# A fused recurrent-attention and mixture-of-experts layer: group 0 enters the pipeline half by half

## The reference, cut to what matters

```
# layer 1, over each group
h = layernorm(x);  h = h / max(norm(h), 1e-12) * sqrt(256) * gamma
q, kv, a = split(h @ w_qkva.T, 3);  a = sigmoid(a)
y[t] = a[t] * y[t-1] + kv[t];       x = x + q * y
# layer 2, top-2 routing to 8 experts, capacity 256 per group and expert
logits = layernorm(x) @ router_w     # softmax, two best, positions by cumsum
hidden = gelu(rows @ w0[e]) * (rows @ w1[e]);  x = x + sum of gate * (hidden @ wo[e])
```

## Time and profile before

| what | before |
|---|---|
| median of three runs | 1752.66 us (1750.37 to 1752.70) |
| the profiled execution's own time | 1755.55 us |
| its span | 1753.8 us |
| busy PE / DVE / ACT / POOL | 1693.2 / 833.6 / 713.8 / 388.6 us |
| mean granted TensorE clock | 0.977 |

### The profile page before, as it was taken

How to read it: one execution, slowest core, us unless ns; L and a number is a source line. 1 busy time by engine, 2 the same in 40 slices (tenths; PEclk the granted TensorE clock), 3 DMA queues, 4 the chain that set the end, 5 groups by cost and what they waited for, 6 DMA issues and landing times.

```text
span 1753.8 us, 25482 instructions
## 1 busy us (share of the span) xinstructions
PE 1693.2 (97%) x10284; PEld 1514.3 (86%) x10284; DVE 833.6 (48%) x1672; ACT 713.8 (41%) x1236; POOL 388.6 (22%) x310
## 2 busy tenths in 40 slices
PE   5989996999999999999999999999999999999997
PEld 4778885989999988899899899899899989989886
DVE  5888875333533354335433453345334533353332
ACT  4556552333533343334433443344333433353332
POOL 3366756411011111111111111111111111111111
PEclk9988986999999999999999999999999999999999
DMA  9356533211411151115111421132113311241111
GB/s 310 131 170 214 194 104 134 59 25 22 116 26 24 25 121 25 25 25 113 33 25 25 97 49 25 25 88 58 25 25 74 72 25 25 53 93 16 34 13 13
DMA packets 112318, 120.76 MB, mean 69 GB/s; under 512 B 14472, under 2 KB 99912, under 8 KB 112200
## 3 DMA queue, kind: packets, MB, share of 16 engines
q1 hardware_dynamic: 87624, 85.29, 16.3%
q0 software_dynamic: 24576, 33.83, 11.3%
HBM read 59.84 MB, written 59.24 MB: 68 GB/s over the span
## 4 chain that ended last, share of the span: by engine, by line
PE 87%; DVE 4%; POOL 4%; ACT 2%; issue 2%; DMA 1%; SPq 0%; POOLq 0%; ACTq 0%
PE bank L1156 53%; PE bank L1172 28%; PE bank L1020 3%; POOL slots L522 2%; PE bank L1096 2%; DVE y L783 1%; POOL pw L506 1%; PE bank L1066 1%; DVE st L803 0%; DVE z L789 0%; PE bank L1056 0%; ACT x2nT L619 0%; POOL sc L510 0%; POOL out L571 0%; ACT xn L594 0%
## 5 line engine op out<-in xcount | busy, mean ns | idle before, releaser
L981 DVE TENSOR_TENSOR y<-bank,sig 128x512 f32<-128x512 f32 (+1 forms) x352 | 243.3, 691 | 571.1 <-PE bank L1156 561.2
L571 POOL DMA_INDIRECT out<-xring x128 | 200.9, 1569 | 1221.4 <-ACT xring L726 1189.8
L709 ACT ACTIVATE hhi<-y 128x512 fp32r<-128x512 f32 (+1 forms) x352 | 222.3, 631 | 525.4 <-DVE y L981 525.4
L1156 PE MATMUL bank<-xThi,whi 128*128 128x512 f32 x1408 | 426.1, 383 | 0.0
L1156 PE MATMUL bank<-xTlo,whi 128*128 128x512 f32 x1408 | 425.4, 382 | 0.0
L1156 PE MATMUL bank<-xThi,wlo 128*128 128x512 f32 x1408 | 423.8, 381 | 0.0
L1172 PE MATMUL bank<-whi,hhi 128*128 128x256 f32 (+1 forms) x1408 | 389.7, 277 | 0.0
L1172 PE MATMUL bank<-wlo,hhi 128*128 128x256 f32 (+1 forms) x1408 | 387.8, 275 | 0.0
L1172 PE MATMUL bank<-whi,hlo 128*128 128x256 f32 (+1 forms) x1408 | 387.4, 275 | 0.0
L984 DVE TENSOR_TENSOR hlo<-y,hhi 128x512 fp32r<-128x512 f32 (+1 forms) x352 | 243.6, 692 | 245.6 <-ACT hhi L709 245.6
L703 ACT ACTIVATE sig<-bank 128x512 f32<-128x512 f32 (+1 forms) x352 | 209.3, 595 | 289.8 <-PE bank L1156 289.8
(11 more groups left out here) (110 smaller groups left out, 1072.0 us busy)
## 6 DMA issues: line engine op xcount, KB each, us to landing
stage<-in_L_ffn_w_kernel SPq DMA_DIRECT2D x160, 128.0 KB, 3.0
slots<-fill SPq DMA_DIRECT2D x32, 520.0 KB, 6.1
xring<-slots SPq DMA_DIRECT2D x32, 520.0 KB, 3.5
stage<-in_L_ffn_wo_kernel SPq DMA_DIRECT2D x80, 128.0 KB, 3.0
xring<-in_L_attn_x SPq DMA_DIRECT2D x16, 512.0 KB, 4.4
out<-xring SPq DMA_DIRECT2D x16, 512.0 KB, 4.1
slots<-rows,sloti POOLq DMA_INDIRECT x128
out<-xring POOLq DMA_INDIRECT x128, 3.8
```

The lines of the kernel that those rows point to most:

```text
L571: pool.indirect_dma_start(out_rows, bass.IndirectOffsetOnAxis(idx, 0), ysb[:, t % 2, j, :], None, compute_op=ALU.add).then_inc(added, 16)
L709: act.activation(hhi[0:n, hc % 3, :], hf[0:n, hc % 2, :], ACT.Copy).then_inc(h_hi, 1)
L981: dve.tensor_tensor(hf[0:n, hc % 2, :], up[hc % 2][1][0:n, :], gel[0:n, hc % 2, :], ALU.mult).then_inc(mul_done, 1)
L1156: last = pe.matmul(lines(up[hc % 2][w][:, :]), (whi, wlo)[wp][:, hc, at:at + P], lines((xThi, xTlo)[xp][:, t % 2, k, :]), start=m == 0 and ...
```

## The change

Group 0's statistics are finished per half: the operands ve of a half are made right behind its bn_aggr, POOL makes a power of 8 columns per half (`powers1_first`), and DVE makes the factors per half (`factors1_first`). In step -1 PE now transposes only half 0 of group 0; half 1 is transposed in step 0, behind `projection(0,0,0)`. Step -1 is written apart for ACT and DVE (`first_step`). DVE takes the statistics of (1,1) in step 0, behind the first recurrence. SP loads the projection weights between the two halves of group 0, ahead of gamma and router. The waits of ACT, DVE and PE for gamma and router stand at their first use. ACT runs one small sigmoid at its start.

```diff
 # SP
             load_x(Turn(0), 0)
+            sync.dma_start(wraw, w_qkva.rearrange("(c p) d -> p c d", p=P)).then_inc(wq_loaded, 16)
             load_x(Turn(0), 1)
             sync.dma_start(gamma[:, :], ...).then_inc(consts_loaded, 16)
             sync.dma_start(router[:, :, :], ...).then_inc(consts_loaded, 16)
-            sync.dma_start(wraw, w_qkva.rearrange("(c p) d -> p c d", p=P)).then_inc(wq_loaded, 16)
 # POOL
+            def powers1_first(h):
+                pool.wait_ge(consts_made, 1)
+                pool.wait_ge(stats1, h + 1)
+                flat = [a[:, h, :, :].rearrange("p k j -> p (k j)") for a in (pw1, ve1, halves)]
+                pool.tensor_tensor(flat[0], flat[1], flat[2], ALU.pow).then_inc(pow1, 1)
...
-                if S:
+                if S and i.value > -2:
                     powers1(i.plus(2))
+                elif S:
+                    powers1_first(0)
+                    powers1_first(1)
 # ACT
-            act.wait_ge(consts_loaded, 32)
+            act.wait_ge(consts_raw, 3)
+            act.activation(nb2[:, 0, 0:1], halves[:, 0, 0, 0:1], ACT.Sigmoid)
...
+            def first_step():
+                normalise1(Turn(0), 0)
+                projection_weights()
+                act.wait_ge(consts_loaded, 32)
+                split1(Turn(0), 0)
+                normalise1(Turn(0), 1)
+                first_weights(0)
+                split1(Turn(0), 1)
+                first_weights(1)
 # DVE
-            dve.wait_ge(consts_loaded, 32)
-            dve.wait_ge(consts_made, 1)
...
-                if h == 1:
+                if g.value == 0:
+                    dve.tensor_scalar(ve1[:, h, 0, :], mv1[:, h, :, 1], LN_EPS, None, ALU.add)
+                    dve.tensor_scalar(ve1[:, h, 1, :], mv1[:, h, :, 1], float(D), None, ALU.mult).then_inc(stats1, 1)
+                elif h == 1:
...
+            def factors1_first(h):
+                dve.wait_ge(pow1, h + 1)
+                ... (the five instructions of factors1, on half h)
...
+            def first_step():
+                factors1_first(0)
+                projection_weights()
+                dve.wait_ge(consts_loaded, 32)
+                split1(Turn(0), 0)
+                factors1_first(1)
+                dve.wait_ge(consts_made, 1)
+                statistics1(Turn(1), 0)
...
                 if B:
                     split1(i, 1)
                     recurrence(i, 0, 0)
+                if i.value == 0:
+                    statistics1(Turn(1), 1)
 # PE
-            pe.wait_ge(consts_loaded, 32)
...
+                if i.value == -1:
+                    transpose1(Turn(0), 0)
+                    return
...
                 if B:
                     projection(i, 0, 0)
+                if i.value == 0:
+                    transpose1(Turn(0), 1)
```

More of the change, by code:

```diff
@@ L228, in build @@
         fac_chain1 = sem("fac_chain1")
+        first_fac_chain1 = sem("first_fac_chain1")
         stats_chain2 = sem("stats_chain2")
@@ L477, in _ @@
                                pattern=[[1, P]], channel_multiplier=-1)
-            pool.memset(halves[:, :, 0, :], -0.5)
+            pool.memset(halves[:, :, 0, :], -0.5).then_inc(consts_raw, 1)
             pool.memset(halves[:, :, 1, :], 0.5)
@@ L500, in first_weights @@
                                    ALU.subtract).then_inc(w_split0, 1)
+            def powers1_first(h):
[3 more added lines that the diff above has]
+                pool.tensor_tensor(flat[0], flat[1], flat[2], ALU.pow).then_inc(pow1, 1)
             def powers1(g):
-                wait(pool, stats1, g, 1, 1)
+                wait(pool, stats1, g, 1, 2)
                 flat = [a[:, :, :, :].rearrange("p h k j -> p (h k j)") for a in (pw1, ve1, halves)]
@@ L589, in normalise1 @@
             def normalise1(g, h):
-                wait(act, fac1, g, 1, 1)
+                if g.value == 0:
+                    act.wait_ge(fac1, h + 1)
+                else:
+                    wait(act, fac1, g, 1, 2)
                 wait(act, t1, g, 2, h)
@@ L644, in step @@
             def step(i):
+                if i.value == -1:
+                    first_step()
+                    return
                 A, B, C, Dg = live(i, 1), live(i, 0), live(i, -1), live(i, -2)
@@ L659, in step @@
                     normalise1(i.plus(1), 0)
-                if i.value == -1:
-                    projection_weights()
                 for hc in first[0:len(first) // 2]:
@@ L735, in _ @@
             dve.sem_inc(mul_done, FREE_MUL)
-            dve.wait_ge(consts_loaded, 32)
-            dve.wait_ge(consts_made, 1)
             in_stats1 = Chain(dve, stats_chain1, 4)
             in_fac1 = Chain(dve, fac_chain1, 4)
+            in_first_fac1 = Chain(dve, first_fac_chain1, 8)
             in_stats2 = Chain(dve, stats_chain2, 4)
@@ L753, in statistics1 @@
                 in_stats1.link(last)
-                if h == 1:
+                if g.value == 0:
+                    dve.tensor_scalar(ve1[:, h, 0, :], mv1[:, h, :, 1], LN_EPS, None, ALU.add)
+                    dve.tensor_scalar(ve1[:, h, 1, :], mv1[:, h, :, 1], float(D), None, ALU.mult).then_inc(stats1, 1)
+                elif h == 1:
                     dve.tensor_scalar(ve1[:, :, 0, :], mv1[:, :, :, 1], LN_EPS, None, ALU.add)
                     dve.tensor_scalar(ve1[:, :, 1, :], mv1[:, :, :, 1], float(D), None, ALU.mult).then_inc(stats1, 1)
+            def factors1_first(h):
+                dve.wait_ge(pow1, h + 1)
+                in_first_fac1.begin(Turn(0), 4 * h)
+                link = in_first_fac1.link
+                link(dve.tensor_tensor(nrm[:, h, :], pw1[:, h, 0, :], pw1[:, h, 1, :], ALU.mult))
+                link(dve.tensor_scalar(rec[:, h, :], nrm[:, h, :], NORM_MIN, None, ALU.max))
+                link(dve.reciprocal(rec[:, h, :], rec[:, h, :]))
+                link(dve.scalar_tensor_tensor(out=sc1[:, h, :], in0=pw1[:, h, 0, :], scalar=float(D) ** 0.5,
+                                              in1=rec[:, h, :], op0=ALU.mult, op1=ALU.mult))
+                dve.scalar_tensor_tensor(out=nb1[:, h, :], in0=mv1[:, h, :, 0], scalar=-1.0, in1=sc1[:, h, :],
+                                         op0=ALU.mult, op1=ALU.mult).then_inc(fac1, 1)
             def factors1(g):
-                wait(dve, pow1, g, 1, 1)
-                in_fac1.begin(g)
+                wait(dve, pow1, g, 1, 2)
+                in_fac1.begin(g.plus(-1))
                 in_fac1.link(dve.tensor_tensor(nrm[:, :, :], pw1[:, :, 0, :], pw1[:, :, 1, :], ALU.mult))
@@ L1060, in route @@
                 wait(pe, x2nT_done, g, 4, 2 * h + 2)
+                if (g.value, h) == (0, 0):
+                    pe.wait_ge(consts_loaded, 32)
                 wait(pe, shifted if h == 0 else routed, g, 1, 0)
```

## The result

| | before | changed |
|---|---|---|
| median of 6 runs, us | 1752.11 (1750.37 to 1753.77) | 1757.63 (1754.81 to 1760.76) |
| profiled execution, own time / span | 1755.55 / 1753.8 | 1757.49 / 1755.8 |
| ratio to before, 95% interval | | 1.003 (1.002 to 1.004) |
| first matmul of the projections, us | 25.80 | 17.87 |
| y(0,0,0), y(0,0,1), first residual start | 30.27, 34.23, 48.15 | 28.20, 37.68, 52.95 |

The changed kernel is slower by 5.5 us, 0.3%. The table's rows show the course: 7.9 us ahead at the first projection (its row on PE begins at 25.80; the 26.15 of the earlier trace rows is where the chain passes to it, behind the transposes), 2.1 ahead at y(0,0,0), 3.5 behind at y(0,0,1), 4.8 behind at the first residual, and 4.3 behind at the first scatter.

The account below looks back on a forecast made before the run. The experts bind PE from 297 us, so the change acts through the chained pipeline ahead. Terms +2.9, +0.4 and +0.9 sum to +4.2 us, 1756.9 us against the median 1752.66; range 1751.8 to 1760.5.

Parts of the forecast that it names:

- Head: Loads, statistics and normalising ahead of PE's projections: projection (0,0,0) starts at 18.2 instead of 26.15, an 8 us win.
- The sigmoid queued behind half 1: ACT's sigmoid waits behind half 1's split and a weight copy; y(0,0,0) starts at 27.5, win down to 2.8 us.
- The wait for the power: DVE's nrm waits for POOL's group 1 power, 0.1 + 2.94 us behind the moved statistics; y(0,0,1) at 35.7 against 34.23.
- The port: DVE's nrm is blocked beside POOL's split of chunk 1 and ends about 1.7 us late; y(0,0,1) then at 37.4.
- No gap on DVE from y(0,1,0) on: DVE works without idling from y(0,1,0) at 41.75 for 9.3 us; first residual at 51.05 against 48.15, +2.9.
- The clock terms: PE's slower clock: +0.4 us in the first projection (5.8 us), +0.9 us for 12 matmuls behind the pause (bounds 0 to 1.9).
- Rival (b): PE's clock falls in the pauses and the first projection stays slow: +7.2 us, 1759.9; chance 0.11.
- The table load: ACT's table load of 1.28 us ahead of normalising goes, by the row; 2.7 by the skill's page, total 1.4 lower.
- The shift arrives: The pipeline has no fixed date, so a shift at about 48 us arrives whole at the end.
- (c): Rival: DVE's wait is covered and the head's 8 us win is kept: 1744.7; chance 0.07.
- (d): Rival: the shift is swallowed by slack between 50 and 100 us: 1752.7; chance 0.06.
- (a): Rival: nrm is not blocked because DVE gets there first; +1.2, +0.4 and +0.2 give 1754.5; chance 0.26.

Follow-up runs that it names:

- the first experiment: The changed kernel with the statistics of (1,1) back in step -1, behind those of (1,0); ratio 0.9976 to the kernel before.
- both lesser terms out: The changed kernel with POOL's split of chunk 1 ahead of group 1's power and 13 more matmuls on PE in the pause; ratio 1.0001 to the kernel before.
- split ahead: The changed kernel with POOL's split of chunk 1 moved ahead of the power of group 1; ratio 1.0007 to the kernel before.
- PE kept busy: The changed kernel with 20 more matmuls on PE into an unused bank, between pa and pkv of block (0,1,0); ratio 1.0011 to the kernel before.
- x first: The changed kernel with the statistics of (1,1) back in step -1 and the projection weights loaded behind both halves of x; ratio 0.9979 to the kernel before.
- the waits alone: The kernel before with only the gamma and router waits moved to first use and ACT's small sigmoid at its start; ratio 0.997.

## Why the prediction was right, point by point

The forecast was 1756.9, the median is 1757.63; +4.2 us was forecast and +5.5 measured. The mechanism is the one that was forecast. That the two times lie only 0.7 us apart is partly luck: the forecast stood on a median of 1752.66 from three runs, six give 1752.11, and the terms were less exact than the total.

- **Head.** Projections at 18.2, measured 17.87. The 26.15 of before, against which the win was counted, is the chain's number; the first matmul began at 25.80. The weights landed by 6.71 (7.0), half 1 by 8.31 (8.5), xn started at 11.32 (11.8). POOL's power of 8 columns takes 1.68 and 1.64 us, inside the bounds, and is hidden.
- **The sigmoid queued behind half 1.** y(0,0,0) at 27.5 plus the clock's 0.4, measured 28.20. Shown by the experiment that puts the sigmoid first: y(0,0,0) at 21.86, against 25.61 in the kernel that it is built on.
- **The wait for the power,** 3.0 us at nrm: measured 3.01. Its removal is the first experiment.
- **The port.** nrm was put at 1.7 us late, from the row at 99.38; it is 1.6 late, and 0.17 us long with the split moved. The same form of stall came back on nb in the experiment with the sigmoid first. Both agree with the rule of the Trainium skill (SBUF — State Buffer, "Who interferes with whom"). That POOL's power does not block agrees with the earlier trace rows and not with that rule: sc and nb of half 0, each of two SBUF tiles, ran at 10.92 and 11.12, beside the power of half 1 (10.55 to 12.19), in 0.16 us each, and xn was not late.
- **No gap on DVE from y(0,1,0) on.** This was wrong. I had the residual 9.3 us behind it; it came 10.96 behind, with idle time of 1.07 ahead of z and 0.83 ahead of xTlo (rows at 44.33 and 45.86 above). Most of it is the clock term, listed apart at 0.9: with both lesser terms out and PE at full clock the stretch took 9.4 (39.15 to 48.55). But a gap of 0.83 at this place needs no half clock. It stands in the kernel before too, where the stretch took 9.96 (38.19 to 48.15), and could have been read there:

```profile
41.05 1.41 DVE L775 SCALAR_TENSOR_TENSOR xTlo<-bank,gamma,xThi 128x512 fp32r<-128x512 f32 x2 [0.83 <-ACT xThi L602]
```

- **The clock terms were too small.** The first projection took 6.7 us against 5.8 forecast, the pause cost 1.9 to 2.2 against 0.9. I had taken middles between bounds; both came at the far side. For the first projection that is chance: nobody edited it, and in the ten other traces without small matmuls ahead of it, that of the kernel before among them, it took 5.5 to 7.1 us (6.9 in the changed kernel's second run, 5.8 with the split ahead, whose head is the same). Rival (b) was right about the mechanism and, with +7.2, too high as a sum; of its two terms the second came whole.
- **The table load.** xn now follows nb at once (nb from 11.12 for 0.16, xn at 11.32), where before the load stood between them and xn came 1.30 us behind its start (15.42 to 16.72): the load was worth the row's 1.28 us, not the 2.7 that the Trainium skill (ScalarE: Activation LUTs, "What ACT_TABLE_LOAD costs") has for load and drain.
- **The shift arrives.** 4.8 us at the residual, 4.3 at the first scatter, 5.5 in the medians. Over ten kernels on the other chips the order of the residuals (53.35, 51.44, 48.3 to 48.6, 45.6, 44.2 to 44.7, 42.1 to 39.5) is roughly the order of the ratios (1.003, 1.0011, 1.0001 and 1.0007, 0.9976, 0.9979 and 0.997, 0.9958 to 0.9971), and from the first to the last the residual moves by 13.9 us and the ratio by 0.0072, 12.8 us. The profiled pair does not show it: there 2.2 us are left where the experts start. Rivals (c) and (d) fall; (a) fell with nrm.

Not settled: how much of the 5.5 us comes behind 50 us. Each of these totals carries some 3 us of uncertainty beside differences of 1 to 5.

## What to carry to other kernels

When an instruction is moved in a program of five queues, ask what is made from its result on another engine: the statistics cost 2 us, but their power on POOL took 3, and POOL's next instruction held up DVE for 1.6 more. Fill the idle time that a reordering opens (6 us on DVE here) before asking another queue to wait. Price a pause of PE with the slower matmuls behind it, which here cost 2 us. And do not count a win at the first matmul (8 us here) before you have followed every engine's queue to the place where the win could be lost again. When two single traces are compared, first take out what no edit caused, here up to 1.5 us of a faster or slower first projection.

## What the runs showed of the hardware

Small bf16 matmuls brought PE's clock up: with 45 of them ahead, transposes that took 1.97 us took 1.09 (rows at 12.12 above and the earlier trace rows), and with 24 more behind these the first projection ran at full clock throughout. Whether the transposes themselves helped is not told apart.

The same pause of PE did not always have the same effect. Ahead of block (0,0,1) PE idled 2.6 us in the changed kernel and in five experiments. The clock stayed up behind it in the changed kernel (twice), in the first experiment and in that with PE kept busy, where the first projection had taken 6.7 to 7.0 us. It fell inside the block in the three where the first projection had been faster (5.6 to 5.8 us: split ahead, both terms out, x first).

On the three other chips every profiled kernel shows PE idle between 300 and 345 us with no releaser, as in the timeline of the kernel with the waits alone, below, and a lower clock around it: the changed kernel ran 273 matmuls at a granted clock of 1.00 in this stretch in its first trace, and 180 at 0.73 in its second. This is absent in the two first traces, and the kernel before takes 27 us more in all on those chips. I did not test its cause.

```profile
309.72 1.01 PE L1162 MATMUL bank<-xThi,whi 128*128 128x512 f32 x2 [0.55 <-issue]
311.14 1.50 PE L1162 MATMUL bank<-xTlo,whi 128*128 128x512 f32 x2 [0.40 <-issue]
...
342.15 0.28 PE L1178 MATMUL bank<-whi,hhi 128*128 128x256 f32 x1 [0.80 <-issue]
```
